# Router scores of the second token half from a kept partial sum, and the second gates earlier in the program

## What is computed

```python
W = weights[condition]                          # x: (64, 64, 1024)
y = jnp.einsum('bct,bcd->bdt', x, W)
xf = y.reshape(-1, 1024)                        # N = 4096 tokens, D = 1024
scores = xf @ Wr.T                              # 64 experts
top_vals, top_idx = jax.lax.top_k(scores, 16)
gates = jax.nn.softmax(top_vals, axis=-1)
G = zeros((N, 64)).at[arange(N)[:, None], top_idx].set(gates)
h = jnp.einsum('nd,krd->nkr', xf, A)            # rank 16
out = jnp.einsum('nkr,kdr->nd', h * G[:, :, None], B)
return x + 2.0 * out
```

## Time and profile before

| | before |
|---|---|
| three timed runs | 721.60, 721.56, 720.78 us; median 721.56 us |
| profiled execution, its own time | 720.82 us |
| its span, first to last instruction | 719.0 us |
| PE busy | 712.3 us (99%) |
| PEld, DVE, ACT, POOL busy | 599.6, 488.6, 262.4, 37.6 us |
| granted TensorE clock, mean | 1.000 |

### The profile page before, as it was taken

The page is one execution under the profiler, slowest core; times in us unless marked ns, Lnnn a source line. Parts: engine busy times, 40 slices in busy tenths (PEclk is TensorE's granted clock), DMA queues, the critical chain, the costliest instruction groups (busy, mean ns, idle before and its releaser), DMA issues.

```text
span 719.0 us, 9267 instructions
## 1 busy us (share of the span) xinstructions
PE 712.3 (99%) x3444; PEld 599.6 (83%) x3444; DVE 488.6 (68%) x953; ACT 262.4 (36%) x499; POOL 37.6 (5%) x30
## 2 busy tenths in 40 slices
PE   9999999999999999999999999999999999999998
PEld 8888887888888888888888888888888888888886
DVE  5698999897546698755343869866534287797652
ACT  5567762534424442133221643122232264223200
POOL 1873000000000000000000000000000000000000
PEclk9999999999999999999999999999999999999999
DMA  9958489755785767475767675845766687545663
GB/s 330 406 198 342 153 301 379 276 223 227 300 321 203 298 240 262 162 255 192 270 242 266 250 291 173 291 167 213 265 233 242 255 308 264 189 147 196 228 220 146
DMA packets 56158, 178.41 MB, mean 248 GB/s; under 512 B 9650, under 2 KB 9778, under 8 KB 55602
## 3 DMA queue, kind: packets, MB, share of 16 engines
q1 hardware_dynamic: 54386, 174.09, 66.6%
q10 hardware_dynamic: 1728, 3.74, 1.4%
HBM read 131.66 MB, written 46.14 MB: 247 GB/s over the span
## 4 chain that ended last, share of the span: by engine, by line
PE 93%; DVE 6%; ACT 0%; issue 0%; POOL 0%; POOLq 0%
PE Pb L267 42%; PE Pb L249 38%; PE Cb L229 7%; PE S L283 4%; DVE Cq L365 2%; DVE Wt L200 1%; DVE Op L182 1%; PE T L522 1%; DVE R L365 1%; PE T L300 0%; PE T L355 0%; DVE Op L545 0%; DVE Xo L182 0%; PE Cb L535 0%; DVE s L333 0%; DVE s L326 0%
## 5 line engine op out<-in xcount | busy, mean ns | idle before, releaser
L249 PE MATMUL Pb<-Op,Wt 128*128 128x512 f32 x1008 | 238.0, 392 | 0.5 <-DVE Op L545 0.5
L249 PEld LDWEIGHTS Pb<-Op,Wt 128*128 128x128 f32 x1008 | 187.6, 188 | 39.2 <-DVE Op L545 0.6
L267 PE MATMUL Pb<-Wt,Op 128*128 128x512 f32 x912 | 212.3, 391 | 1.7 <-DVE Op L182 1.7
L267 PEld LDWEIGHTS Pb<-Wt,Op 128*128 128x128 f32 x912 | 169.9, 188 | 36.6 <-DVE Op L182 2.1
L365 DVE TENSOR_TENSOR Q<-Pb,Q 128x512 f32<-128x512 f32 x112 | 77.4, 691 | 87.7 <-PE Pb L267 87.7
L267 PE MATMUL Pb<-Wt,Ox 128*128 128x512 f32 x432 | 100.8, 391 | 0.0
L235 ACT COPY R<-Cb 128x512 f32<-128x512 f32 x60 | 35.3, 588 | 161.8 <-PE Cb L229 161.8
L267 PEld LDWEIGHTS Pb<-Wt,Ox 128*128 128x128 f32 x432 | 80.5, 188 | 16.3
L182 DVE TENSOR_TENSOR Op<-R,Op 128x512 fp32r<-128x512 f32 x98 | 70.1, 740 | 19.0 <-ACT Op L180 19.0
L365 DVE TENSOR_TENSOR Cq<-Pb,Cq 128x512 f32<-128x512 f32 x64 | 44.0, 688 | 40.9 <-ACT Cq L376 30.9
L249 PE MATMUL Pb<-Ox,Wt 128*128 128x512 f32 x288 | 66.3, 389 | 0.0
(11 more groups left out here) (90 smaller groups left out, 463.7 us busy)
## 6 DMA issues: line engine op xcount, KB each, us to landing
Wt<-Wd SPq DMA_DIRECT2D x168, 512.0 KB, 4.8
Wd<-Wt SPq DMA_DIRECT2D x56, 512.0 KB, 4.2
Q<-in_x SPq DMA_DIRECT2D x32, 512.0 KB, 5.0
xc<-in_x SPq DMA_DIRECT2D x24, 512.0 KB, 4.0
out<-Q SPq DMA_DIRECT2D x32, 256.0 KB, 2.6
out<-Q SPq DMA_DIRECT2D x16, 512.0 KB, 2.9
BR<-in_B SPq DMA_DIRECT2D x3, 1024.0 KB, 8.7
BR<-in_x SPq DMA_DIRECT2D x11, 256.0 KB, 11.2
```

The source lines that it names most:

```text
L249: t = pe.run(lambda e, c=c, o=o, a=a, z=z: e.matmul(Pb[:, b, :], Wt[:, k, a, 128 * c:128 * c + 128], part(o, z), start=fresh and (c, a, z) ...
L267: t = pe.run(lambda e, c=c, o=o, k=k, a=a, z=z: e.matmul(Pb[:, b, :], part(o, a)[:, 128 * i:128 * i + 128], Wt[:, k, z, :], start=fresh an ...
```

## The change

- **First 512 tokens.** The term Wr2 y21 is finished alone, and `s_first` has ACT copy it to `sS`. The term Wr1 y11 is then finished alone, `s_keep` has ACT copy it to `sX` (a place in `xc` in stage 0, in `rest` later), and DVE adds `sX` to `sS`.
- **Second 512 tokens.** Since y12 = T1 + y11, their scores are Wr1 T1 + Wr1 y11 + Wr2 y22. T1 is split anyway. `score` of T1 runs after tile (2, 1), `score` of y22 after (2, 3), and `s_sum` has DVE add `S` and the kept `sX` into `sS`. The splits of y12 (4 casts on ACT and 4 subtractions on DVE in each stage) are gone.
- **Second gates.** In all stages now: `s_turn` after (3, 0), `top_a` before (3, 1), `exps` and `top_b` before (3, 2), `top_c` before (3, 3), `g_turn` after (4, 2). Before, these stood in stage 0 at (3, 2), (3, 3), (4, 0), (4, 1), (5, 0), and in the other stages at (3, 1), (3, 2), (3, 3), (4, 0), (4, 3).
- **Buffers.** One of the two `Xo` buffers, whose place in `xc` now holds `sX`, is no longer handed out.

```diff
--- before.py
+++ after.py
@@ -107,7 +107,7 @@
         with nc.sbuf_tensor("BR", [128, 3, 4, 512], F32) as BR:
             pass
         Ox = sb("Ox", [128, 4, 2, 512], F32R)
-        sb("rest", [128, 2, 1024], F32)
+        rest = sb("rest", [128, 2, 1024], F32)
 
         with nc.sbuf_tensor("xc", [128, 2, 1024], F32) as xc:
             pass
@@ -149,6 +149,7 @@
         raws = [BR[:, 0], BR[:, 1], BR[:, 2], u]
         x0 = [raws[i // 2][:, 2 * (i % 2):2 * (i % 2) + 2, :].rearrange("p a b -> p (a b)") for i in range(8)]
         S2_split = [None] * 4
+        B22_free = []
         Wa = xc[:, 0, :].rearrange("p (v d) -> p v d", d=64)
 
         S2x = [R[:, 1, 4 + c, :] for c in range(4)]
@@ -156,7 +157,7 @@
 
         bank_free, bank_n = [None] * 4, [0]
         cb_free, cb_n = [[None], [None]], [0]
-        op_free, op_spare = [None] * (NO + 6), deque([*range(NO), NO + 4, NO + 5])
+        op_free, op_spare = [None] * (NO + 6), deque([*range(NO), NO + 4])
         w_ready, w_free, w_kept = {}, {}, {}
         w_next = [UNITS]
         t_free, s_free, sS_free, G_free = [None], [None], [None], [None]
@@ -289,9 +290,21 @@
             return t
 
 
-        def s_copy(done):
+
+        sX_free = [None]
+
+        def s_first(done):
             ac.after(done, sS_free[0])
             s_free[0] = ac.run(lambda e: e.copy(sS[:, :], S[:, :]))
+            return s_free[0]
+
+        def s_keep(done, first, sX, *tokens):
+            ac.after(done, *tokens)
+            s_free[0] = ac.run(lambda e: e.copy(sX, S[:, :]))
+            return add(ve, sS[:, :], sS[:, :], sX, s_free[0], first)
+
+        def s_sum(done, sX):
+            s_free[0] = sX_free[0] = add(ve, sS[:, :], S[:, :], sX, done, sS_free[0])
             return s_free[0]
 
         def s_turn(tok):
@@ -581,7 +594,7 @@
                 t2[c] = add(ve if s else gp, y11[c], y22[c], y11[c], split["T1"][c][1], R_ready[1][1], op=ALU.subtract)
 
             def sum_t3(c):
-                t3[c] = add(ve, y12[c], y22[c], y12[c], split["y12"][c][1], R_ready[1][1], op=ALU.subtract)
+                t3[c] = add(ve, y12[c], y22[c], y12[c], t1[c], R_ready[1][1], op=ALU.subtract)
 
             def sum_t4(c):
                 t4[c] = add(ve, y21[c], y21[c], y11[c], split["y21"][c][1], t2[c], R_ready[0][1], op=ALU.subtract)
@@ -602,14 +615,15 @@
             uses = ["y21", "y11", "T1", "y22", "T2", "T3", "T4"]
             early, late = ((0, 1), (2,), (3,), ()), ((), (0,), (1,), (2, 3))
             state = {}
+            sX = rest[:, 0, 0:512] if s else xc[:, 1, 0:512]
+            sX_home = (sX_free[0], *B22_free)
             for m, name in enumerate(FIRST):
                 for j in range(4):
                     step = 4 * m + j
                     weights()
                     if s == 0 and m >= 5:
-                        for k in (NO + 4, NO + 5):
-                            if k in op_spare:
-                                op_spare.remove(k)
+                        if NO + 4 in op_spare:
+                            op_spare.remove(NO + 4)
 
                     if s == 0 and 6 <= step < 10:
                         q = (3, 2, 1, 0)[step - 6]
@@ -625,7 +639,7 @@
                     if more and step in (24, 26):
                         k = (step - 24) // 2
                         if s == 0:
-                            xc_free[k] = op_free[NO + 4 + k]
+                            xc_free[k] = (op_free[NO + 4], sX_free[0])[k]
                         load_x(s + 1, k)
 
                     if s == 0:
@@ -661,18 +675,12 @@
                     elif m == 2:
                         for c in early[j]:
                             need("y22", c)
-                        if s:
-                            for c in late[j]:
-                                need("y12", c)
                         sum_t2(j)
                         if s == 0 and j == 3:
                             for c in range(4):
                                 raw["T3b", c] = add(gp, BR[:, 1, c, :], BR[:, 2, c, :], BR[:, 1, c, :], B_ready[1],
                                                     B_ready[2], op=ALU.subtract)
                     elif m == 3:
-                        if s == 0 and j == 0:
-                            for c in range(4):
-                                need("y12", c)
                         for c in (late if s == 0 else early)[j]:
                             need("T2", c)
                         if j == 1:
@@ -702,29 +710,29 @@
                         raw["D", j] = add(ve, s2_place(j), Cq[:, 1, j, :], Cq[:, 3, j, :], Cq_ready[1][j], Cq_ready[3][j],
                                           *((u_busy[j],) if s else (split["y22"][j][1], t2[j], t3[j])), op=ALU.subtract)
 
-                    if (m, j) in ((1, 2), (3, 3 if s == 0 else 2)):
+                    if (m, j) in ((1, 2), (3, 1)):
                         state["nm"] = top_a(state["t"])
-                    if (m, j) in ((1, 3), (4, 0) if s == 0 else (3, 3)):
+                    if (m, j) in ((1, 3), (3, 2)):
                         state["exps"] = exps(state["nm"])
                         state["b"] = top_b()
-                    if (m, j) in ((2, 0), (4, 1) if s == 0 else (4, 0)):
+                    if (m, j) in ((2, 0), (3, 3)):
                         state["c"] = top_c(state["b"], state["exps"])
 
                     b, done = first(base + 4 * m + j, split[uses[m]], j == 3, name not in CHAIN)
                     if (m, j) == (0, 1):
                         pe.after(wr_ready)
-                        score(split["y21"], 1, True, False)
+                        state["s"] = s_first(score(split["y21"], 1, True, True))
                     if (m, j) == (1, 0):
-                        state["s"] = s_copy(score(split["y11"], 0, False, True))
-                    if (m, j) in ((1, 1), (3, 2 if s == 0 else 1)):
+                        state["s"] = s_keep(score(split["y11"], 0, True, True), state["s"], sX, *sX_home)
+                    if (m, j) in ((1, 1), (3, 0)):
                         state["t"] = s_turn(state["s"])
                     if (m, j) == (2, 3):
                         g_turn(state["c"], 0)
-                    if (m, j) == (3, 0):
-                        score(split["y22"], 1, True, False)
-                    if (m, j) == (3, 1 if s == 0 else 0):
-                        state["s"] = s_copy(score(split["y12"], 0, False, True, True))
-                    if (m, j) == ((4, 3) if s else (5, 0)):
+                    if (m, j) == (2, 1):
+                        score(split["T1"], 0, True, False)
+                    if (m, j) == (2, 3):
+                        state["s"] = s_sum(score(split["y22"], 1, False, True), sX)
+                    if (m, j) == (4, 2):
                         g_turn(state["c"], 1)
                     drain_first(name, j, b, done)
                     if s == 0:
@@ -770,6 +778,7 @@
                             u_busy[c] = t
                         elif m == 5:
                             op_free[NO + c] = t
+                            B22_free.append(t)
                     if m == 0:
                         gated(0, c, 0)
                         need("G11", c)
```

## The result

| | before | changed |
|---|---|---|
| median of six runs | 721.23 us | 726.52 us |
| lowest to highest | 720.72 to 721.60 us | 726.42 to 728.51 us |
| profiled execution, its own time | 720.82 us | 728.51 us |
| its span | 719.0 us | 726.7 us |
| mean granted clock, profiled execution | 1.000 | 0.995 |

The account below looks back on a forecast made before the run. PE bounds the kernel, busy for 712.3 of 719.0 us. The terms +2.6, +3.4 and -1.7 make +4.3 on 720.82, 725.1; with 0.4 added for the median, 725.5 us, range 722.3 to 728.0.

Parts of the forecast that it names:

- PE's own work: All stages: the same 32 score matmuls and four groups of four transposes per stage, costed at 0.
- First term: Stage 0: first scores' transposes wait for DVE's kept sum behind a weight split, +2.6 us, range 1.45 to 2.7.
- Second term: Stage 0, after E (tile (3, 0) ends on PE): PE waits for T2 block 2 behind DVE's queue, +3.4 us.
- Third term: Stage 0's first gated product: PE's old 1.68 us wait for DVE's split of the last block goes whole, -1.7 us.
- The missing splits: Stage 0, second gates: the four y12 splits gone lay where DVE would now idle, so they buy nothing there.
- the clock falls in a wait: Behind 3.4 us of idle PE, matmuls run slow, costing 2.1 us, for 727.6 us; chance 0.10.

Follow-up runs that it names:

- t3_sums_earlier: Changed kernel with the four T3 sums of stage 0 one tile earlier in DVE's queue, at (3, 0); 722.86 us, ratio 1.0027.
- gates_late: Changed kernel with the second gates of stage 0 where they were before the change; 723.43 us, ratio 1.0041.
- difference_and_late: by_difference with the edit of gates_late; 721.39 us, ratio 1.0004.
- best_guess: by_difference with the edit of t3_sums_earlier and, in stage 0, exps and top_b at (4, 0), top_c at (4, 1), g_turn at (5, 0); 720.23 us, ratio 0.9986.
- best_split: best_guess with the first four match_replace of top_b in stage 0 at (3, 2), the rest at (4, 0); 719.30 us, ratio 0.9975.
- turn_later: Changed kernel with stage 0's first-score transposes and top_a, exps, top_b, top_c of the first gates one tile later; 724.68 us, ratio 1.0041.
- by_difference: Changed kernel with y11 scores accumulated onto the y21 scores, whose copy is put aside, and DVE subtracting, in all stages; 724.70 us, ratio 1.0053.
- kept_sum_alone: Kernel before with the kept sum of stage 0 added and one Xo buffer fewer; 724.96 us, ratio 1.0046.

## Why the prediction was right

The forecast was 725.5 us, range 722.3 to 728.0, slower with 0.84; measured 726.52. Step by step:

- **PE's own work, 0.** Right: 3444 matmuls in both, and stages 1 to 3 take 516.7 us in both.
- **First term, +2.6, between 1.45 and 2.7.** Right in place and cause: the wait is there, for that sum, behind that weight split. Its size is not one number. The profiles have 2.88, 2.8, 1.9 and 1.8 us, and the sum itself 1.74 or 0.68. The forecast took one end; both occur. Counted as the forecast did, to the start of the transposes, the changed kernel's profile has 45.52 - 42.54 = 3.0 us, 0.3 above the range of the term, because the weight split started 0.3 us later than before.
- **Second term, +3.4.** Right nearly to the row: DVE resumed at E + 2.57 (forecast 2.56), block 2 was written at E + 13.37 (13.35), and the wait is 3.16 us as idle time, 3.4 from start to start. t3_sums_earlier shows that it is DVE's queue.
- **Third term, -1.7.** Right: DVE comes to the old place 6.5 us later and PE 9.7, so DVE gains 3.2 us on PE (3.0 forecast), which turns a wait of 1.8 us into a lead of 1.4. The wait is back whenever the second gates stand late (gates_late, difference_and_late).
- **The missing splits, 0.** Nothing measurable in difference_and_late, whose old wait is as long as before, as forecast. best_guess and best_split gain with the T3 sums in their place. Whether moving `top_a` and part of `top_b` alone would gain in the kernel before was not tried.
- **The clock.** This is the step that was weighed wrongly. The rival "the clock falls in a wait" had a chance of 0.10 and a price of 2.1 us; the sum had it at nothing. The price was a little high: 1.6 and 1.7 us per fall in the changed kernel's profile, 1.6 to 1.7 in those of turn_later, by_difference and kept_sum_alone. It was worked out from the slow opening, whose clock column prints 1.00. The chance was far too low: the mean clock is 0.998 or less in all six executions. From start to start, one fall with the shorter first wait gives 721.2 + 2.0 + 3.4 - 1.8 + 1.6 = 726.4, the usual time; two falls with the longer one give 720.8 + 3.0 + 3.4 - 1.8 + 1.6 + 1.7 = 728.7, about the profiled execution's 728.5. That the unprofiled ones are of the first kind is inferred from their times; they left no trace.

So the forecast came within 1 us partly by luck: if the usual execution is as inferred, the first term was 0.6 us too large and the missing clock 1.6 us too small.

The Trainium skill ("TensorE: Matmul & The Clock Gate", section "Why this matters for your kernels") warns of long idle gaps on PE between bursts of matmuls, because the clock drops behind them. The traces agree: none has a fall behind a wait of 1.7 to 1.9 us, and falls come behind 2.8 to 3.2 us, though by the mean clocks not in every execution.

## What to carry to other kernels

Where the main engine hardly ever waits, as here, more work elsewhere costs nothing and less gains nothing (difference_and_late has four splits fewer per stage and the same time); what costs is an instruction that is put ahead of another in a queue with little lead. Count, for each consumer, when its producer's queue reaches the split it needs, and spend what a change frees in the idle time just ahead of that point. And price a new wait of some 3 us on PE with the slow matmuls that can come behind it, 1.6 to 1.7 us more per fall here.

## What was not expected

- The lower clock after a wait of 2.8 or 3.2 us, in some executions and not in others, from one kernel: kept_sum_alone (2.8) and turn_later (3.2) have both groups. In turn_later they lie 2 us apart, and it spreads over 2.5 us, where the kernel before beside it spreads over 1.5.
- A DVE sum of two SBUF tiles that lasts 0.68 or 1.74 us in the same place of the program, as POOL is past its last sum or not. Where it stands on the path, an execution can be 1 us longer or shorter by it.
- An opening whose length differs by up to 1.1 us between executions (7.52 to 8.63) and moves all that follows. With it, the waits from start to start (the short ones near 34 to 36 us too, where they occur) and the measured slow stretches, the profiled executions of the changed kernel and of the experiments on stage 0 add up to within 0.2 us of their times.
